# A decoder layer on one core: the attention input loaded twice, work moved from GpSimd to VectorE and ScalarE, and a new order of steps

## What is computed

```
n  = layernorm(x);  q, k, v = split(n @ w_attn.T)                  # 16 heads of 16
y  = causal linear attention(elu(q)+1, elu(k)+1, v)
x1 = x + (y @ w_proj.T)
# cross attention on probabilities of layernorm(x1) and ctx
qp, kp = prob(layernorm(x1)), prob(ctx)                            # tanh, then shares of the row sum
s  = softmax(-(qp - kp) @ (log qp - log kp).T / 16)
f  = (ctx - s @ ctx) @ W_diff.T + b_diff + layernorm(x1)
o  = layernorm(gelu(layernorm(f) @ W1.T + b1) @ W2.T + b2 + f)
x2 = x1 + o
# a block on the 128 tokens of each row with the highest router score
h  = layernorm(x2);  idx = top128(h @ w_router)
z  = h[idx] + attention(rmsnorm(h[idx]));  z = z + gated ffn(rmsnorm(z))
out = x2 + h, with z in place of h at the rows idx
```

## Time and profile before

| | us |
|---|---|
| median of 3 runs | 922.85 |
| lowest and highest | 919.57, 923.87 |
| the profiled execution | 919.85 |
| its span, first to last instruction | 918.0 |
| TensorE busy | 817.0 (89%) |
| VectorE busy | 725.8 (79%) |
| ScalarE busy | 577.3 (63%) |
| GpSimd busy | 301.5 (33%) |

### The profile page before, as it was taken

How to read it: one execution, slowest core, us unless ns; L and a number is a source line. 1 busy time by engine, 2 the same in 40 slices (tenths; PEclk the granted TensorE clock), 3 DMA queues, 4 the chain that set the end, 5 groups by cost and what they waited for, 6 DMA issues and landing times.

```text
span 918.0 us, 21136 instructions
## 1 busy us (share of the span) xinstructions
PE 817.0 (89%) x7222; PEld 705.6 (77%) x7222; DVE 725.8 (79%) x1609; ACT 577.3 (63%) x1550; POOL 301.5 (33%) x443
## 2 busy tenths in 40 slices
PE   6788798999989898999989898999989898988875
PEld 4567578888888788888888788888888788867654
DVE  5767778888898979888897979888897979766452
ACT  5363449576666849576675849576675848564742
POOL 0031515234251525234251524234251524224121
PEclk8789899999999999999999999999999999999999
DMA  8310101111020101101020101101020101101010
GB/s 292 84 47 1 59 24 47 41 35 48 6 81 6 57 29 46 40 29 51 6 80 6 57 29 46 40 29 51 6 80 6 57 29 46 30 2 46 6 53 7
DMA packets 26871, 39.82 MB, mean 43 GB/s; under 512 B 2256, under 2 KB 18768, under 8 KB 26832
## 3 DMA queue, kind: packets, MB, share of 16 engines
q1 hardware_dynamic: 23344, 28.74, 9.4%
q0 software_dynamic: 2048, 6.30, 2.3%
q10 hardware_dynamic: 1440, 4.28, 1.4%
HBM read 24.62 MB, written 14.70 MB: 43 GB/s over the span
## 4 chain that ended last, share of the span: by engine, by line
PE 35%; DVE 22%; issue 17%; POOL 11%; ACT 10%; DMA 3%; POOLq 1%; SPq 0%; DVEq 0%; ACTq 0%
PE bank L1117 10%; DVE a_s L867 4%; PE bank L1239 3%; ACT w_raw_or_stage_c L712 3%; PE bank L1221 2%; DMA x_in<-in_x 2%; PE bank L1301 2%; ACT L712 2%; PE bank L1309 2%; PE bank L1401 2%; PE bank L1279 2%; PE bank L1385 2%; PE bank L1396 2%; POOL f_rs L436 1%; DVE prob L908 1%
## 5 line engine op out<-in xcount | busy, mean ns | idle before, releaser
L675 ACT ACTIVATE prob<-bank,b_folded 128x256 f32<-128x256 f32 x128 | 53.8, 471 | 111.4 <-PE bank L1117 111.2
L867 DVE TENSOR_TENSOR a_s<-bank,const 128x512 f32<-128x512 f32 x112 | 72.6, 685 | 40.0 <-PE bank L1239 21.7
L712 ACT ACTIVATE w_raw_or_stage_c<-bank,c_nmax 128x128 f32<-128x128 f32 x256 | 91.7, 406 | 3.2 <-DVE c_nmax L1037 3.0
L451 POOL TENSOR_TENSOR a_tr_lo<-a_norm,a_tr_hi 128x512 fp32r<-128x512 f32 x16 | 20.6, 1285 | 141.2 <-ACT a_tr_hi L562 141.2
L712 ACT ACTIVATION_READ_ACCUMULATOR w_raw_or_stage_c<-bank,c_nmax 128x1 f32 x256 | 62.7, 245 | 0.0
L784 DVE TENSOR_TENSOR b_s_lo<-prob,b_s_hi 128x512 fp32r<-128x512 f32 x64 | 44.9, 701 | 17.3 <-ACT b_s_hi L562 17.3
L427 POOL TENSOR_TENSOR q_bias<-b_f,vectors_by_row 128x512 f32<-128x512 f32 x16 | 20.6, 1285 | 114.4 <-DVE b_f L933 114.4
L1037 DVE TENSOR_REDUCE c_nmax<-bank 128x4 f32<-128x512 f32 x64 | 41.1, 685 | 21.0 <-PE bank L1401 21.0
L857 DVE RECIPROCAL a_e<-a_e 128x512 f32<-128x512 f32 x16 | 53.5, 3346 | 0.0
L537 POOL DMA_INDIRECT out<-w_raw_or_stage_c,row_of_slot_out x16 | 17.5, 1091 | 95.9 <-DVE w_raw_or_stage_c L1085 95.9
L1117 PE MATMUL bank<-b_s_hi,w_mlp_hi 128*128 128x256 f32 x256 | 45.1, 298 | 2.7 <-ACT prob L675 1.4
(11 more groups left out here) (254 smaller groups left out, 2729.2 us busy)
## 6 DMA issues: line engine op xcount, KB each, us to landing
token_rows<-norm_x_rms SPq DMA_DIRECT2D x16, 513.0 KB, 4.0
x_in<-in_x SPq DMA_DIRECT2D x16, 256.0 KB, 3.0
qc<-in_ctx SPq DMA_DIRECT2D x16, 256.0 KB, 2.7
b_f<-in_ctx_t SPq DMA_DIRECT2D x16, 256.0 KB, 2.7
out<-w_raw_or_stage_c SPq DMA_DIRECT2D x16, 256.0 KB, 2.2
w_raw_or_stage_c<-in_w ACTq DMA_DIRECT2D x4, 512.0 KB, 5.9
w_raw_or_stage_c<-in_w_gu ACTq DMA_DIRECT2D x4, 341.0 KB, 3.1
w_raw_or_stage_c<-in_w_a SPq DMA_DIRECT2D x2, 384.0 KB, 4.6
```

Source lines behind the costliest of these rows:

```text
L675: act_in(prob[:, 2 * (j % 2) + n, :], b0[:, n * T:(n + 1) * T], ACT.Gelu, bias=b1p[:, f:f + 1]).then_inc(b_gelu.sem, 1)
L712: act_in(c_e[g % 2][:, j * R:(j + 1) * R], C_SCORES[g][:, j * R:(j + 1) * R], ACT.Exp, bias=c_nmax[:, n:n + 1], accum_out=c_den[:, head:he ...
L867: tt(heads(A_MASKED[t][n][:, :]), heads(A_SCORES[n][:, :]), tri.unsqueeze(1).broadcast_to([P, 4, P]), ALU.mult).then_inc(a_scput.sem, 1)
```

## The change

Four parts of the computation move, and the order table is a new one.

1. `x1` is no longer copied from `x_in` by GpSimd (`a_kept`). SyncE loads x a second time, from DRAM into `x1` (`keep_x`), once `b_kept` and `b_normed` of the row before have read it.
2. `out` rows: GpSimd computed x2 + h. Now ScalarE computes x2·(1 + rstd) - mean·rstd, two activations with a scale and a bias per partition, from three tiny GpSimd operations (`c_obs`).
3. `a_ylo` moves from GpSimd to VectorE.
4. `c_etput_0..3` move from ScalarE to VectorE.
5. `ORDER` and `WARM_AT` are new: 69 warming matmuls in rounds in place of 72.

```diff
 ORDER = """
-c_w2 a_kput+ c_ff_0++ c_ff_1++ c_gtlo_1++ c_rstd+ c_ht+ a_score_0+ b_fput+ b_fmean+ b_htp+ a_sput+ c_hsc+
...
+c_w2 b_frstd+ c_gthi_0++ c_gtlo_0++ c_ob+ b_fput+ b_fmean+ c_gthi_1++ a_kput+ a_sput+ b_fd+ c_gtlo_1++ c_hsc+
...
+            sp.dma_start(x1[:, :, :], x_rows[0]).then_inc(a_kept.sem, 16)
...
             def next_x(b):
                 sp.wait_ge(*a_normed(b))
                 sp.sem_inc(passed.sem, 1)
-                sp.wait_ge(*a_kept(b))
+                sp.dma_start(xin[:, :, :], x_rows[b + 1]).then_inc(x_in.sem, 16)
+
+            def keep_x(b):
+                sp.wait_ge(*b_kept(b - 1))
                 sp.sem_inc(passed.sem, 1)
-                sp.dma_start(xin[:, :, :], x_rows[b + 1]).then_inc(x_in.sem, 16)
+                sp.wait_ge(*b_normed(b - 1))
+                sp.sem_inc(passed.sem, 1)
+                sp.dma_start(x1[:, :, :], x_rows[b]).then_inc(a_kept.sem, 16)
...
                 store(i - 2)
+                keep_x(i)
                 next_ctx_t(i - 1)
...
-            def a_kept_(b):
...
-                nc.gpsimd.tensor_copy(x1[:, :, :], xin[:, :, :]).then_inc(a_kept.sem, 1)
...
-            def c_ob_(b):
-                pool.wait_ge(*c_normed(b))
-                if not first(b):
-                    pool.wait_ge(*out_done(b - 1))
-                nc.gpsimd.tensor_tensor(ob[:, :, :], x2, c_norm, ALU.add).then_inc(c_ob.sem, 1)
+            def c_obs_(b):
+                pool.wait_ge(*c_rstd(b))
+                if not first(b):
+                    pool.wait_ge(*c_ob(b - 1))
+                pool.sem_inc(passed.sem, 1)
+                nc.gpsimd.tensor_scalar(c_gain[:, :], c_rs[:, :], 1.0, None, ALU.add).then_inc(c_obs.sem, 1)
+                nc.gpsimd.tensor_tensor(c_offset[:, :], c_mv[:, :, 0], c_rs[:, :], ALU.mult).then_inc(c_obs.sem, 1)
+                pool.wait_ge(*c_obs(b, 2))
+                pool.sem_inc(passed.sem, 1)
+                nc.gpsimd.tensor_scalar(c_offset[:, :], c_offset[:, :], -1.0, None, ALU.mult).then_inc(c_obs.sem, 1)
...
+            def c_ob_(b):
+                act_e.wait_ge(*c_obs(b))
+                if not first(b):
+                    act_e.wait_ge(*out_done(b - 1))
+                for t in range(TT):
+                    act_in(ob[:, t, :], x2[:, t, :], ACT.Identity, bias=c_offset[:, t:t + 1], scale=c_gain[:, t:t + 1]) \
+                        .then_inc(c_ob.sem, 1)
...
+            def c_etput_(g):
+                def step(b):
+                    dve.wait_ge(*c_etp(b, g + 1))
+                    nc.vector.tensor_copy(c_et[g], EXP_T[g][:, :]).then_inc(c_etput.sem, 1)
+                return step
```

## The result

| | before | after |
|---|---|---|
| median | 922.73 us (4 runs) | 887.66 us (4 runs, 886.99 to 888.36) |
| ratio | | 0.9625, 95% interval 0.960 to 0.965 |
| span of the profiled execution | 918.0 | 886.5 |

The forecast was 914.6 with a range of 903 to 929: right in its direction, and wrong by 27 us, outside the range. By the spans, 31.5 us went where I had seen 6.7. Of these 24.8 us, 16.0 lie in the 13 rounds and 8.8 in the two ends.

The account below looks back on a forecast made before the run. VectorE's chain was taken to bound A, TensorE B (with two waits) and C. Thirteen rounds at -0.67 gave -8.7, ends +2.0, sum -6.7: 913.2 or 916.2 by base, forecast 914.6, range 903 to 929.

Parts of the forecast that it names:

- C: TensorE without holes: From a_score_0 to the next b_o, 24.28 us: TensorE works 24.21 and is the bound; VectorE has room.
- B: TensorE with two holes: From c_idx to a_score_0, 12.62 us: TensorE waits only twice, 0.55 for c_idxput and 0.80 for a_phi_k.
- A: VectorE's chain: From b_o to c_idx, 14.80 us: VectorE, busy 13.65, is the bound and TensorE waits for it.
- Part A: b_o to c_idx: copies +1.80, b_vq +0.60, collisions at b_diff -0.76 and c_sel -0.65, f_rs wait -0.31; +0.68 a round.
- Part B: c_idx to a_score_0: TensorE's new order removes its waits for c_idxput and a_phi_k, -1.35 us a round.
- both waits have work in front of them: c_idx to a_score_0: moved TensorE work covers the waits; c_idxput must be 0.8 us late, a_phi_k 2, to show.
- Part C: a_score_0 to next b_o: VectorE's added 1.55 us fits in its 1.91 of idle time, so 0.
- The ends: Start and end of the kernel: x load +0.5, last row's c_pick about +2.0, ScalarE's removed copies -0.5; +2.0 us.
- Rival 1: c_hx on GpSimd still holds c_sel, the round loses 0.65 of its 0.67; about 923 us, chance 0.18.
- Rival 2: Copies land on VectorE while b_diff and c_sel still wait; round longer by 0.74, 933 us, chance 0.12.
- Rival 3: b_kept on GpSimd waits for ScalarE's late c_ob, then b_htp; round loses 0.5, about 921 us, chance 0.10.
- Rival 4: Copies hide wholly, b_o to c_idx shrinks to TensorE's need; round near 49.9, about 900 us, chance 0.08.

Follow-up runs that it names:

- pool_clean2: Kernel before with GpSimd's c_ob, b_kept and b_qb moved later, x loaded a second time, and SyncE's loads ahead of store and keep_x; 896.45 us.
- vq_late: Changed kernel with b_vq on VectorE moved from ahead of c_rank to behind c_idxput; 894.75 us.
- c_order: Kernel before with two VectorE moves: a_mean behind a_scput_3 and b_hlo behind a_scput_1; 911.81 us.
- clean_c: pool_clean2 with two VectorE moves added: a_mean behind a_scput_3 and b_hlo behind a_scput_1; 892.88 us.
- order_old_work: Kernel before with the new order table, the work staying on its old engines; 922.30 us.
- ob_back: Changed kernel with the out rows back on GpSimd as one add ahead of b_kept, without the tiny operations and the two activations; 896.34 us.
- rms_first: Changed kernel with c_rms1 directly behind c_rstd, ahead of c_h2rms, on GpSimd; 893.34 us.
- hybrid: Changed kernel with the four c_etput copies back on ScalarE and the stretch from b_o to c_idx in the old order; 900.31 us.
- hybrid2: hybrid with b_onormed ahead of c_dinv and c_keep again, one VectorE move; 892.88 us.

## Why the forecast was wrong, step by step

**What bounds the kernel.** "C: TensorE without holes" failed: 0.3 us of stall lay under modelled ends. "B: TensorE with two holes" named the sign and not the cause. "A: VectorE's chain" held only as long as the collisions lasted: with them gone (pool_clean2) `c_sel` is ready 0.85 before `c_idx`.

**Part A, +0.68, measured -0.07.** This is the largest miss of the round, 0.75 us of it against 0.38 in C and 0.24 in B. My sum took 1.41 off for two collisions and 0.31 for `f_rs`, and put 2.40 on for three copies and `b_vq`, each at its full length. Clearing GpSimd alone gives -0.57 (pool_clean2), so all the rest of the change together costs +0.50 in A where my other terms add up to +2.09. So the charge for the added work is the term of A that was mis-sized. Along VectorE the starts say where. Right: the three copies (0.60, 0.54 and 0.61 from start to start, 1.75 for 1.80), `b_diff` -0.77 for -0.76, the wait for `f_rs` -0.31, `c_sel` -0.79 for -0.65. Missing: what the copies and tiny steps save by standing between dependent neighbours (start to start, before less after): `b_omean` 0.11, `b_onormed` 0.13, `c_dinv` 0.08, `c_mean` 0.08, `c_keep` 0.15, `c_normed` 0.12, in all **-0.67**, read from the starts of either trace; a new wait of 0.39 at `c_o` in place of one of 0.23 gives 0.15 back. Only the first kind was looked at by a run, and one that was not clean; the size is read, not proven by experiment. And `b_vq`'s 0.60 should not have been charged: `c_rank` waits for `c_sbc` on TensorE, and without `b_vq` ahead of it VectorE stands idle for 0.67 there (vq_late).

**Part B, -1.35, measured -1.59.** The number is near by luck, and the mechanism is the step that failed: "both waits have work in front of them". The two moves on TensorE are worth +0.07 alone and +0.29 with GpSimd cleared. What pays is VectorE, 1.04 earlier in B because `b_ratio` and `a_phi_q` are no longer stretched, plus what it brings from A: together -1.21 (pool_clean2). The cost that I put at nothing is these two collisions. I had the earlier trace rows for `b_diff` and `c_sel` and did not compare the medians of the other VectorE instructions with two SBUF inputs.

**Part C, 0, measured -0.38.** The added work was hidden, as forecast. The new order of `a_mean` and `b_hlo` was an edit that I did not price at all (-0.3 in c_order, -0.13 on top of the cleared GpSimd in clean_c).

**The ends, +2.0, measured -6.8.** `x1`: 0.5, right. `c_pick` of the last row: 7.80 behind its `c_normed` against 7.00, +0.8 for +2.0, with the transfers on the chain that ends last now. Chain of the changed kernel, the end:

```profile
843.35 3.63 DMA token_rows<-norm_x_rms
...
847.77 3.64 DMA picked_rows<-token_rows,row_of_slot
```

What shortens the end is before that: the last `c_normed` starts 52.0 behind the last `b_v`, before it was 55.8. The cleared GpSimd has little of it (55.4 in pool_clean2), nor has the new table with the old work (55.9 in order_old_work); which part of the change gives it is open. The start goes with the clock in these traces. Busy time by stretch, start and end, of before, after and c_order:

```profile
0.00:144.67 144.67, 116.85 (x898) 91.07 (x899) 103.15 (x204) 69.31 (x150) 33.44 (x51) 0.91 0.24 81
816.15:918.00 101.85, 74.22 (x552) 58.42 (x552) 49.01 (x125) 48.96 (x154) 26.40 (x43) 0.95 0.08 26
```

```profile
0.00:141.15 141.15, 113.69 (x904) 90.71 (x904) 103.92 (x214) 72.63 (x163) 29.67 (x50) 0.93 0.27 88
787.97:886.50 98.53, 72.26 (x549) 56.13 (x547) 49.23 (x130) 43.31 (x135) 24.48 (x45) 0.99 0.08 27
```

```profile
0.00:138.66 138.66, 111.51 (x898) 85.78 (x899) 103.55 (x204) 69.22 (x150) 34.15 (x51) 0.95 0.26 84
```

Nearly the same matmuls keep TensorE busy for 116.85, 113.69 and 111.51 us at granted clocks of 0.91, 0.93 and 0.95, and the starts are 144.67, 141.15 and 138.66 long. In pool_clean2, at 0.88, TensorE is busy for 119.89 us, and the start is 145.94 long, so the collisions are not what makes it long. Why the clock was lower in one than in another was not tried. My term for the start, +0.5, had nothing of this. The profiles with the changed kernel's table, or a few steps of it moved, have their third `b_v` at 139.3 to 141.4, the two hybrids at 144.0 and 144.4.

**The rivals.** Rival 1 (a collision remains) did not happen, but five of my own kernels fell into one (order_old_work, ob_back, rms_first, hybrid, hybrid2). Rival 2 needs collisions that were gone. Rival 3 happens in the old table only. Rival 4, "more is won, a round near 49.9, about 900", came nearest in its number and had a chance of 0.08. Its mechanism, that the copies hide wholly and A shrinks to what TensorE needs, is not what happened: A is only 0.07 shorter, and the gain is in B and C. Had I priced four collisions on VectorE, VectorE would have had 2.6 us a round to win in A and B, and it would have been the likeliest.

## What to carry to other kernels

When one instruction is stretched by a neighbour engine, list shortest and median duration of every instruction of that kind: two of the four collisions here were in instructions that I had not compared. A wait on the bound engine names who released it, not why that one was late; moving the waiter passes the wait on, unless what it waits for comes earlier. And a table that is moved as a whole must be priced as a whole: with three engines within half a us, moving one to four of its steps cost 6 to 24 us here, and no such move made the changed kernel faster.

## What the runs showed of the hardware

- GpSimd and a VectorE instruction with two SBUF inputs hold each other up, in both directions. A 128x512 VectorE difference takes 0.69 alone and 1.24 to 1.45 beside a GpSimd add. An add of 128x256 that starts 0.03 earlier is enough (hybrid2, 1.25), and `a_kq`, 128x512 as well, lasts 2.17 where an indirect DMA issue and an add follow each other on GpSimd (ob_back). The other way round, the first operation of `c_rms1`, 128x2, takes 1.31 in the changed kernel, while VectorE goes from `c_normed` through `b_diff` into `c_rscore`, against 0.20 in the kernel before.
- A VectorE instruction that takes one of its two inputs from PSUM is not held in these traces. In the kernel before, the first half of `c_rank` (414.77) takes 0.47 while `c_hx` runs on GpSimd from 414.25 to 415.47, and it takes 0.47 in the changed kernel with no add beside it. `b_vq` (416.84) takes 0.68 while `b_kept` starts at 416.94, and `b_kept` takes 1.27, both as long as elsewhere.
- A `tensor_scalar` from bf16 to bf16 in SBUF (`c_sel`, one tensor input) is held as well: 0.41 for the pair alone, 0.83 behind `c_hx` in rms_first. The Trainium skill, "SBUF — State Buffer", section Who interferes with whom, names `tensor_scalar` among those that can take the shared ports; these rows agree.
- A stall of about 0.2 us behind a group of 16 matmuls showed as no idle time; the distance between the starts showed it, 1.89 before and 1.70 in c_order.
